# Second expert layer of a one-core kernel: the groups in another order, tables and blank rows earlier, half of the dense gates inside the tile loop

## The reference, cut to what matters

```
def ffn(x):                       # x is normalised before the call
    xn     = layernorm(x) * gamma + beta
    abel   = gelu(xn @ abel_w + abel_b)            # the "dense branch", 256 -> 256
    logits = xn @ moe_gate_w + moe_gate_b          # 256 -> 8 experts
    topw, topi = top_k(logits, 2); topw = softmax(topw)
    moe = sum over the two chosen experts of topw * (gelu(xn @ ew1[e] + eb1[e]) @ ew2[e] + eb2[e])
    moe = moe @ expm(g0) @ expm(g1) @ expm(g2)
    gate = sigmoid(concat(abel, moe) @ gc_w + gc_b)
    return x + abel * (1 - gate) + moe * gate
```

## Time and profile before

| | before |
|---|---|
| median of three runs | 1361.19 us |
| profiled execution, first to last instruction (span) | 1360.3 us |
| busy: PE, DVE, POOL, ACT | 1172.3, 861.9, 412.5, 495.3 us |
| mean granted PE clock | 0.931 |

### The profile page before, as it was taken

One profiled execution on the slowest core, in us unless ns is written; L12 is line 12 of the kernel. 1 busy time (PEld: TensorE's weight loads), 2 busy tenths in 40 slices (PEclk: granted clock), 3 DMA queues, 4 the chain that ended last, 5 costly groups with the idle time before them and its releaser, 6 DMA issues.

```text
span 1360.3 us, 26013 instructions
## 1 busy us (share of the span) xinstructions
PE 1172.3 (86%) x7280; PEld 1018.5 (75%) x7281; DVE 861.9 (63%) x2756; ACT 495.3 (36%) x967; POOL 412.5 (30%) x480
## 2 busy tenths in 40 slices
PE   6796878986899999973699989999992999999958
PEld 5673656874788889962589877888881888989947
DVE  6536677876566666655876668767546566666646
ACT  1010553442434444431233333334451444444435
POOL 3001111577344444430000000104555344444410
PEclk9898997787999999996899999998996999999989
DMA  8500123354444533324011011001237443533357
GB/s 284 169 0 8 63 89 114 132 199 160 148 136 132 180 108 89 89 84 178 0 48 47 2 47 47 1 1 59 100 123 232 159 119 114 166 108 101 112 184 252
DMA packets 72271, 149.15 MB, mean 110 GB/s; under 512 B 10918, under 2 KB 36210, under 8 KB 72186
## 3 DMA queue, kind: packets, MB, share of 16 engines
q1 hardware_dynamic: 51626, 92.87, 19.8%
q0 software_dynamic: 19776, 54.45, 13.1%
q10 hardware_dynamic: 784, 0.79, 0.2%
HBM read 82.63 MB, written 65.44 MB: 109 GB/s over the span
## 4 chain that ended last, share of the span: by engine, by line
PE 60%; issue 7%; DVE 6%; DMA 4%; POOL 2%; ACT 2%; SPq 1%; POOLq 1%; DVEq 0%; ACTq 0%
PE bank L2150 17%; PE bank L1694 8%; PE bank L1695 8%; PE bank L1696 7%; PE bank L1564 6%; PE bank L1720 4%; PE bank L1773 2%; PE bank L1703 2%; PE bank L2208 2%; DMA xh<-slots_in 2%; PE bank L188 1%; POOL xh L1356 1%; DVE work L1933 1%; DVE xs L1920 1%; PE bank L2161 1%
## 5 line engine op out<-in xcount | busy, mean ns | idle before, releaser
L1694 PE MATMUL bank<-ew,rows 128*128 x852 | 298.0, 350 | 4.5 <-DVE rows L1230 2.4
L1695 PE MATMUL bank<-low_in,rows 128*128 x852 | 273.6, 321 | 0.0
L1696 PE MATMUL bank<-ew,rows 128*128 x852 | 272.3, 320 | 0.0
L1367 POOL DMA_INDIRECT results<-xh x142 | 141.8, 998 | 293.1 <-DVE xh L1258 274.0
L1694 PEld LDWEIGHTS bank<-ew,rows 128*128 128x128 f32 x852 | 161.6, 190 | 15.4 <-issue 8.0
L1696 PEld LDWEIGHTS bank<-ew,rows 128*128 128x128 f32 x852 | 161.1, 189 | 11.5
L1695 PEld LDWEIGHTS bank<-low_in,rows 128*128 128x128 f32 x852 | 162.0, 190 | 6.0
L1531 ACT ACTIVATE xh<-bank 128x512 f32<-128x512 f32 x142 | 85.0, 598 | 217.7 <-PE bank L1696 217.7
L1267 DVE TENSOR_TENSOR rows<-bank,rows 128x512 fp32r<-128x512 f32 x142 | 98.2, 691 | 95.0 <-ACT rows L200 95.0
L1346 POOL DMA_INDIRECT slots_in<-xh,work x120 | 118.0, 983 | 81.4 <-DVE work L1127 47.7
L636 POOL TENSOR_TENSOR work<-work,mhalf 128x8 f32<-128x8 f32 (+1 forms) x22 | 38.7, 1760 | 316.7 <-DVE work L629 316.6
(11 more groups left out here) (334 smaller groups left out, 2031.7 us busy)
## 6 DMA issues: line engine op xcount, KB each, us to landing
xh<-slots_in POOLq DMA_DIRECT2D x142, 129.0 KB
low_in<-low SPq DMA_DIRECT2D x32, 512.0 KB
xh<-results SPq DMA_DIRECT2D x14, 1032.0 KB, 5.5
dense<-ab SPq DMA_DIRECT2D x12, 512.0 KB, 4.8
xs<-in_L_attn_a_x_dram SPq DMA_DIRECT2D x4, 1024.0 KB
ew<-in_L_ffn_ew_dram SPq DMA_DIRECT2D x2, 2048.0 KB, 14.3
ew<-in_L_ffn_ew_dram SPq DMA_DIRECT2D x4, 1024.0 KB, 13.6
low<-xh SPq DMA_DIRECT2D x8, 512.0 KB, 2.7
```

What stands on the lines that cost most here:

```text
L1367: pool.indirect_dma_start(out=yg, out_offset=bass.IndirectOffsetOnAxis(ap=back[j % RING], axis=0), in_=yr[j % RING], in_offset=None).then_ ...
L1694: pe.matmul(o, hi, f32r(high(c)), start=(c == 0), stop=False)
L1695: pe.matmul(o, hi, f32r(low(c)), start=False, stop=False)
L1696: last = pe.matmul(o, lo, f32r(high(c)), start=False, stop=(stop and c == chunks[-1]))
```

## The change

It touches the second expert layer alone (r == 1); the first keeps its order.

- `ORDER` becomes 3, 0, 4, 5, 6, 7, 1, 2: the groups still to be routed stand at steps 0 and 2 to 5, groups 1 and 2 at steps 6 and 7.
- `count_all`, the totals, stands right behind the last routed group's `rank`, ahead of the last two dense products.
- SP writes the blank rows ahead of the stores of groups 1 and 2 and loads the weights of experts 1, 2 and 3 only behind those; expert 0's are loaded earlier.
- DVE makes the tables right after the last `locate`, then the gates of groups 1 and 2. The gates of groups 5, 6 and 7 (12 instructions) stand two by two in steps 1 to 6 of the tile loop, and the tokens' weights (`token_weights`, three small operations) in step 6.

```diff
-            ORDER = [3, 0, 4, 1, 5, 2, 6, 7] if r == 1 else list(range(NG))
+            ORDER = [3, 0, 4, 5, 6, 7, 1, 2] if r == 1 else list(range(NG))
+            ROUTED = 1 + max(p for p, g in enumerate(ORDER) if g >= EARLY_GROUPS)
+
+            GATED = [1, 0, 2, 6, 7, 3, 4, 5] if r == 1 else list(range(NG))
+            gated = lambda g: GT * (GATED.index(step_of[g]) + 1)
...
-                LATE = {NG - 4: (0,), NG - 3: (1,), NG - 2: (2, 3)} if r == 0 else {NG - 3: (0,), NG - 2: (1,), NG - 1: (2, 3)}
+                LATE = {NG - 4: (0,), NG - 3: (1,), NG - 2: (2, 3)} if r == 0 else {NG - 4: (1,), NG - 3: (0,), NG - 2: (2,)}
+                IN_LOOP = (3, 4, 5) if r == 1 else ()
...
+                else:
+                    for p in range(ROUTED, NG):
+                        dense_gate(ORDER[p])
+
+                in_loop = [(ORDER[p], t) for p in IN_LOOP for t in range(0, GT, 2)]
+
+                def aside(j):
+                    if isinstance(j, int) and 1 <= j <= len(in_loop):
+                        g, t = in_loop[j - 1]
+                        dense_gate(g, range(t, t + 2))
+                    if r == 1 and isinstance(j, int) and j == len(in_loop):
+                        token_weights()
+                        v.wait_ge(zab_ok, NT)
...
                     if not is_last(j):
                         route_back(j + 1, k + 1, turn + (k + 1) // RING)
-
+                    aside(j)
...
-                EARLY = 2
+                EARLY = 2 if r == 0 else 1
...
+                    if r == 1 and p == ROUTED:
+                        sp.wait_ge(tables_ok, TAILS)
+                        pad()
                     if ORDER[p] < LOWS:
                         spill(p)
-                        if p >= 3:
-                            fetch_weights(p - 3 if r == 0 else (p - 3) // 2)
+                        if r == 0 and p >= 3:
+                            fetch_weights(p - 3)
+                        if r == 1 and ORDER[p] == 0:
+                            fetch_weights(0)
...
+                    if r == 1 and p == ROUTED:
+                        count_all()
```

More of the change, by code:

```diff
@@ L1140, in vector, with dense_gate @@
             def vector(v):
-                def dense_gate(g):
+                def dense_gate(g, some=range(GT)):
                     v.wait_ge(gelu_ok, step_of[g] + 1)
[L1144 to L1147, removed]
+                    for t in some:
+                        after(v, zab_ok, gated(g) - GT + t)
+                        v.scalar_tensor_tensor(prod, ab[:, g * GT + t, :], 1.0, gcw[:, 1, :], ALU.mult, ALU.mult,
+                                               accum_out=zab[:, g * GT + t:g * GT + t + 1]).then_inc(zab_ok, 1)
                 def rest_late(n):
@@ L1211, in vector, with token_weights @@
                 v.tensor_scalar(done, tincl, float(out_past), None, ALU.add).then_inc(tables_ok, 1)
[L1213 to L1219, removed]
-                        rest_late(2 + p - NG // 2)
-                for n in range(2 + NG // 2, LATE_FOLDS):
-                    rest_late(n)
-                v.wait_ge(zab_ok, NT)
+                def token_weights():
+                    v.wait_ge(ed_ok, 1)
+                    then(v, v.tensor_scalar(wts[:, :, 0], dtop, 1.0, None, ALU.add))
+                    then(v, v.reciprocal(wts[:, :, 0], wts[:, :, 0]))
+                    then(v, v.tensor_tensor(wts[:, :, 1], dtop, wts[:, :, 0], ALU.mult))
+                if r == 0:
+                    token_weights()
+                    for p in range(NG // 2, NG):
+                        dense_gate(ORDER[p])
+                        rest_late(2 + p - NG // 2)
+                    for n in range(2 + NG // 2, LATE_FOLDS):
+                        rest_late(n)
+                    v.wait_ge(zab_ok, NT)
+                else:
+                    for p in range(ROUTED, NG):
+                        dense_gate(ORDER[p])
+                in_loop = [(ORDER[p], t) for p in IN_LOOP for t in range(0, GT, 2)]
[4 more added lines that the diff above has]
+                    if r == 1 and isinstance(j, int) and j == len(in_loop):
+                        token_weights()
+                        v.wait_ge(zab_ok, NT)
                 def copy_x(j, k, turn):
@@ L1403, in store_fold, with pad @@
                     sp.dma_start(low2[e][:, hs.start * C:hs.stop * C], late_rest[n % 2].rearrange("p h c -> p (h c)")).then_inc(late_st[n % 2], 16)
+                def pad():
+                    for e in range(E):
+                        at = sp.value_load(tails[0:1, e:e + 1], min_val=e * REGION, max_val=e * REGION + T)
+                        sp.dma_start(xg[bass.ds(at, P), :], zero[:]).then_inc(padded, 16)
                 for p in range(NG):
@@ L1417, in sync @@
                         store_fold(p - NG + 2)
-                sp.wait_ge(tables_ok, TAILS)
-                for e in range(E):
-                    at = sp.value_load(tails[0:1, e:e + 1], min_val=e * REGION, max_val=e * REGION + T)
-                    sp.dma_start(xg[bass.ds(at, P), :], zero[:]).then_inc(padded, 16)
+                if r == 0:
+                    sp.wait_ge(tables_ok, TAILS)
+                    pad()
                 for n in range(2, LATE_FOLDS):
@@ L1634, in dense, with count_all @@
                     last.then_inc(ab_ps, 1)
+                def count_all():
+                    pe.wait_ge(run_ok, NG)
+                    pe.wait_ge(lg_ok, NG)
+                    pe.matmul(bank[:, 6, 0:E], onesb[:], run[NG % 2], start=True, stop=True).then_inc(rank_ps, 1)
                 if r == 0:
@@ L1663, in tensor @@
                         turn_late(p - NG + ALONG)
-                pe.wait_ge(run_ok, NG)
-                pe.wait_ge(lg_ok, NG)
-                pe.matmul(bank[:, 6, 0:E], onesb[:], run[NG % 2], start=True, stop=True).then_inc(rank_ps, 1)
                 if r == 0:
+                    count_all()
                     fold_late(ALONG - 1)
```

4 lines of the change are left out of this document (2 added, 2 removed).

## The result

| | before | changed |
|---|---|---|
| median, and range, of six runs each on one chip | 1361.72 us (1359.12 to 1366.22) | 1355.43 us (1352.81 to 1358.09) |
| profiled execution: span | 1360.3 us | 1352.5 us |
| busy: PE, DVE, POOL, ACT | 1172.3, 861.9, 412.5, 495.3 us | 1170.6, 860.8, 413.5, 496.5 us |
| mean granted PE clock | 0.931 | 0.934 |

The ratio is 0.9937, 95% interval 0.9914 to 0.9959: 6.3 us faster. The forecast was 5.5 us. The engines are busy as long as before, so what went is standing still.

The account below looks back on a forecast made before the run. PE bounds the tile loop, so its 22.95 us idle ahead of it can shrink. Scatters 2.8 plus landing 3.5 minus gates 0.8 gives 5.5 us: span 1354.8, median 1355.7 us, range 1353.0 to 1359.2.

Parts of the forecast that it names:

- Scatters: Second routing on POOL: 32 scatters run without waiting for slots, ending at 1038.85, 2.8 us earlier.
- The prediction's count: DVE's slots for groups 5, 6 and 7 out at about 1005.6, 1012 and 1018.5, ahead of POOL's need.
- Landing: Last scatter's end to first load: 3.1 us as in the first routing instead of 6.7; 3.5 us gained.
- Load to PE: First load to PE's first row stays at 2.39 us, so PE starts at 1044.35.
- Gates in the loop: Steps 1 to 6 of the tile loop: gates and token weights on DVE delay `up`, costing 0.8 us.
- a granted clock under 1: Sign that the forecast is wrong: PE's granted clock below 1 in the loop's first eight tiles.
- Rival (d): Stores of groups 1 and 2 reach into the last scatters and slow the load 1 to 2 us; 1357.3 us; 10%.
- Rival (a): Scatters don't hold the first load; tables and blank rows decide, 15 us less, some 1346 us; 3%.
- (b): Tile loop pays for gates and a PE clock drop, 8.1 us together; 1363.0 us, slower than before; 6%.
- (c): Half the gain: gates cost 3 us, or a late slot ends scatters at 1041 as before; 1358.5 us; 16%.
- (e): No shortening: PE stands still as long as before, scatters' landing taking 6.7 us here too; within 0.2%; 5%.
- the forecast 6.3: PE's start of the tile loop comes 6.3 us earlier: 2.8 us from scatters, 3.5 us from landing.

Follow-up runs that it names:

- both pairs of the table: Two side-by-side traces of the kernel before and the changed kernel, one on chip A, one on chip D; spans differ by 7.8 and 8.8 us.
- the first pair: Kernel before and changed kernel, each profiled once on chip A: spans 1360.3 and 1352.5 us.
- the second: Kernel before and changed kernel profiled again side by side on chip D: medians 1365.51 and 1354.51 us.
- the three kernels traced on chip D: Changed kernel, 1354.51 us; it with group 4 routed at step 1, 1354.12; that with rank products ahead of the next group's logits, 1354.28.
- chip D: Chip of the last four runs: kernel before 1365.51 us, changed kernel 1354.51 us, ratio 0.9922.
- chip A: Chip of the main comparison: kernel before 1361.72 us, changed kernel 1355.43 us, ratio 0.9937.
- the two kernels whose scatters end closer to the stores: Changed kernel with group 4 routed at step 1, 1354.12 us; the same with rank products ahead of the next group's logits, 1354.28 us; both chip D.
- Chips B and C: Slower chips of the first eight experiments: kernel before 1400.28 and 1398.33 us; changed kernel 1396.43 us on C, ratio 0.9991.
- old order with early blank rows: Kernel before, its group order kept, tables ahead of gates and blank rows ahead of expert 1's weights: 1399.35 us, 0.9988; again 1396.66 us, 0.9999.
- group 4 first: Changed kernel with group 4 routed at step 1, ahead of group 0: 1396.8 us, 0.9975; chip C 1391.58 us, 0.9949; chip D 1354.12 us, 0.9936.

## Why the prediction was right

It forecast 1355.7 us in a range of 1353.0 to 1359.2; the median is 1355.43. Step by step, with both pairs of the table:

- **Scatters, 2.8 us forecast: 4.2 and 4.1 measured.** The 32 scatters took 40.46 and 40.44 us without a pause, as forecast (40.9, which had 0.6 us for slowed ones in it). The kernel before took 45.49 us for them in the first pair and 46.41 in the second, so 5.0 and 6.0 us were saved. Against that stands group 4's later start behind the logits, forecast at 1.8 us and measured at 0.83 and 1.85. The first is small because the kernel before had there already paid as much in another way: its 16 dense products at 988.92 ran at a lower granted clock and took 5.38 instead of 3.69 us, and the changed kernel's ran at full clock. In the second pair the same products of the kernel before ran at full clock (3.69 us at 991.09, granted clock 1.00), and the price was the forecast 1.8. What was mis-sized there is the saving: scatters of 1.06 to 1.22 us, beside the full DMA engines, had made the row of before longer (46.41), and none of them remained. So the term was 1.4 and 1.3 us too small, for a different reason in each pair.
  DVE had the slots of groups 5, 6 and 7 out at 1002.24, 1008.85 and 1014.72, where POOL wanted them at 1005.91, 1016.02 and 1026.12. The prediction's count (1005.6, 1012, 1018.5) was over 3 us late, on the safe side. It also took the low clock at 988.92 to follow a wait of 0.37 us; the same wait stands at 1002.18, and there the products took 3.69 us. So the wait alone doesn't explain it.
- **Landing, 3.5 us forecast: 3.8 and 4.7 measured.** The first routing's 3.1 us was a good stand-in; it became 2.89 and 2.83 us. The price of before varies (6.66 and 7.53 us), so the gain does. The size was right and the reason only in part: the prediction put the 3.6 us down to the blank rows. The rows above show DMA engines filled by stores and weights, which slowed the scatters as much as the blank rows; the change helped because it moved expert 1's weights too.
- **Load to PE, no change forecast:** 2.42 and 2.52 us, against 2.39 and 2.45.
- **Gates in the loop, 0.8 us forecast: 0.49 and 0.22 measured.** One placement of the gates varies by more: with them in the loop it took 259.33 to 260.29 us in the three kernels traced on chip D. So only a bound is shown, about 1 us. DVE's and PE's timelines show the mechanism, as in the earlier trace rows:

```profile
1056.72 0.22 DVE L1263 SCALAR_TENSOR_TENSOR xh<-xh,work 128x1 int32<-128x1 f32 x1
1056.86 0.42 DVE L1149 SCALAR_TENSOR_TENSOR work<-ab,gcw 128x256 bf16<-128x256 f32 x1
1057.20 0.08 DVE L1149 DVE_READ_ACCUMULATOR work<-ab,gcw 128x1 f32 x1
1057.32 0.43 DVE L1149 SCALAR_TENSOR_TENSOR work<-ab,gcw 128x256 bf16<-128x256 f32 x1
...
1057.69 0.42 DVE L1251 SCALAR_TENSOR_TENSOR rows<-bank,rows 128x256 fp32r<-128x256 f32 x1
```

```profile
1074.19 0.49 PE L1732 MATMUL bank<-ew,rows 128*128 x1 [0.36 <-DVE rows L1251]
```

  Two gates stand between the row numbers and the copy, 0.83 us with their ends overlapped. Only the step with the tokens' weights shows PE waiting for that copy: 0.36 us here, 0.76 in the other trace of the changed kernel. The delays don't add up tile by tile, as forecast. The sign "a granted clock under 1" in the first eight tiles was badly chosen: in both kernels on chip A the clock is 0.50 in the first 3.5 us of the loop, behind PE's long idle, and 1.00 from 7 us on.
- **Rival (d), the first load slowed by the stores:** not in this kernel (2.89 us). Something of that size, 1.2 us, appeared in the two kernels whose scatters end closer to the stores. Rival (a), that the scatters don't hold the load, is out by the chain, (b) by the loop's length, (c) and (e) by POOL's row and PE's idle.
- **Sum:** 7.9 and 8.8 us were gained up to PE's first row, 1.6 and 2.4 more than the forecast 6.3. The medians show 6.3 us less, and 10.9 on chip D. That the forecast of the median came within 0.3 us is partly luck: a start gain under-sized by 1.6 us, and runs that spread over 5 us.

## What to carry to other kernels

When the chain names one releaser, look at every other producer of the same wait: here the blank rows and the scatters were late together, and each was named in one of two traces of the same kernel. When two transfers are late together, look at the DMA share too: here the engines were full with other transfers issued just ahead, and once those were elsewhere the blank rows landed in 2.3 us (median) and the last scatter in 2.5. Most of the 17 us by which the blank rows moved lay behind the scatters' end and bought nothing. In an in-order queue, ask what each entry waits for: blank rows behind stores that wait for the last gelu cost 15 us on a chip where that gelu was late. Cut two traces of each kernel at the same instruction: both pairs showed the start 8 to 9 us sooner, where the medians said 6.3 and 10.9. For a term under 1 us two traces were not enough. And run the parts of a change on the chip that showed its gain: here they met slower chips, and the split stayed open.

## What the hardware showed that was not expected

**A gate beside a result scatter lengthens the scatter, not the gate.** Durations (min/median/max, ns) of POOL's result scatters in the changed kernel, first in the six steps with gates, then behind them, and of the gates:

```profile
L1390 POOL DMA_INDIRECT results<-xh x6: 1183/1248/1263, 1053.4 to 1071.7; - x6
```

```profile
L1390 POOL DMA_INDIRECT results<-xh x10: 997/997/1000, 1076.1 to 1109.2; - x10
```

```profile
L1149 DVE SCALAR_TENSOR_TENSOR work<-ab,gcw x28: 417/424/461, 1002.1 to 1072.2; 128x256 bf16<-128x256 f32 x28
```

With the gates ahead of the loop, the first six of these scatters (chip C, where the changed kernel's first six have a median of 1252 ns):

```profile
L1391 POOL DMA_INDIRECT results<-xh x6: 1000/1000/1011, 1097.9 to 1116.5; - x6
```

That is 0.25 us each, and POOL has it to spare (busy 0.43 of the loop). The two kernels differ in the gates' place, so the lengthening comes with them. The gates didn't wait: the twelve in the loop took 417 to 426 ns, as in the earlier trace rows; the one of 461 stands in the routing, at 1009.69. The GPSIMD Engine Reference of the Trainium skill (Specifications) says that POOL shares its SBUF interfaces with DVE and contends with DVE instructions that have two SBUF inputs. The trace agrees that the two disturb each other. The prediction had asked whether a gate would wait for a scatter, up to 6 us in all; that didn't happen. That the shared interface is the cause is not shown by a run.

**Chips B and C took 37 to 39 us more than chip A for the kernel before, and on C, where the changed kernel ran as well, the change gave nothing that could be measured.** The loop took the same 259 to 262 us. What can be seen of the difference lies in code that is written out: in the old order of groups, group 3's first scatter came at 1000.88 (C) and 1005.08 us (B) instead of 977.83. ACT stood still with its input ready. In the changed kernel on chip C, PE had finished the transposes at 1045.16 and the dense product at 1055.04:

```profile
1054.54 1.02 ACT L205 ACTIVATE work<-bank 128x1024 f32<-128x1024 f32 x1 [6.05 <-remote]
...
1063.12 1.02 ACT L1539 ACTIVATE ab<-bank 128x1024 f32<-128x1024 f32 x1 [7.56 <-remote]
```

SP's own small steps between two transfers took 0.7 us apiece at first and less than half of that later in the same list (chain of the old order with early blank rows, chip C):

```profile
1061.46 0.71 SPq L1421
...
1072.32 0.27 SPq L1421
```

On these chips the load starts 4.6 us or more behind the scatters, with blank rows that take 8 to 19 us to issue. A change to the scatters can still gain there: group 4 first gained 4.85 us on chip C. Why the changed kernel gained nothing is not settled, and why these engines stand still is open; no run was made for it.
